# edge_mlp's own term on ScalarE with one row added in PSUM; the attention stages' value sums on TensorE and their keys laid by ScalarE; stage loads in order of need

## The chip, the cores and the metric

One core of a Trainium2 chip runs the whole program in one launch. The metric is the device time of one execution in microseconds (us). The kernel before takes 4426.26 us, the median of three runs (4425.43 to 4427.96).

## What is computed

Four graph layers over 3,125 nodes with 256 features and 53,125 edges, sorted by destination node. `h` is the rectified layer norm of `x`, and each layer adds its result to `x`.

```python
# layer 0: message MLP, node MLP, layer norm
m     = relu(concat([h[src], h[dst], edge_attr]) @ eW1 + eb1) @ eW2 + eb2
agg   = segment_sum(m, dst)
x    += layer_norm(h + relu(concat([h, agg]) @ nW1 + nb1) @ nW2 + nb2)
# layer 1: 4 heads; the key of an edge carries its relation
enh   = h + 0.1 * query_emb
score = sum_d(Q[dst] * (K[src] + 0.2 * rel_w[edge_type])) / 8
w     = softmax over the edges of a destination
x    += layer_norm(segment_sum(w * V[src], dst) @ Wo + bo + h)
# layer 2: 8 heads, a softmax over all edges, key + edge_attr @ We
# layer 3: graph attention with one head, then gates (tanh, sigmoid)
```

## The kernel before

The nodes are ordered and cut into 25 blocks of 128, one node per partition. The edges of a node are taken four at a time: a *step* handles one block with up to four edges ("slots", QE = 4) for each of its 128 nodes. There are 120 steps in each edge stage, 15 turns of a hardware loop with AQ = 8 steps. A step's record (`rec`) holds its block number and the source nodes of its four slots.

The stages run one after the other with a barrier between: lists, tables for layer 0 (`make_tables`), `edge_mlp`, `update_nodes`, `attend` for layer 1, `project_out`, `attend` for layer 2, `share_softmax`, tables for layer 3, `gat_edges`, `gate_nodes`. Five engines run their own written orders, tied only by semaphores; there is no scheduler. `Chain` makes VectorE (DVE) wait for its own last instruction (`step(...)`), or lets it go on and wait later (`put`, `until`). `hold` is a wait and a no-op. In a step GpSimd (POOL) issues indirect DMAs: four gather the source rows of the four slots from a table in HBM (512 values a row) into `ring`, and in `edge_mlp` and layer 2 a fifth gathers edge features. SyncE (SP) loads the records, and waits until a ring slot is free before it does.

`edge_mlp` (lines 1058 to 1171) makes, for each slot, relu(source row + the block's own row + features times `w_edge`) and adds the four into the block's accumulator in `S["big"]`. TensorE (PE) turns the features (L1130, L1131), writes the own row (with bias, 512 wide, in `S["big2"]`) into the slots 0, 1 and 2 of `psX` by a product with the identity (L1135), and adds the feature products (L1142). `psX` has one PSUM bank for each slot. DVE adds the own row of slot 3 (L1161), adds `psX` to the ring two slots at a time (L1163), and rectifies and sums (L1170). ScalarE (ACT) only copies the turned features (L1118).

`attend` (lines 1512 to 1796) keeps a running maximum `m`, sum `l` and weighted values in `S["big"]` for each block. In step k PE makes the edges' keys in `psX[k % 2]` from the turned features (L1688) and adds the gathered keys with the identity (L1693). DVE multiplies them with the queries (L1764), reduces to scores (L1770), masks (L1778), takes the maximum (L1782) and subtracts it (L1786); ACT takes the exponential (L1664). DVE handles the values one step later: the values of step k-1 are weighted by those exponentials (L1708), the old sum is decayed (L1715), and the four weighted rows are added up (L1712, and L1719 twice). ACT also copies turned features (L1638), and in layer 1 builds one-hot relations (L1646, L1649).

`update_nodes` and `project_out` run rounds over 25 blocks; `NextTables` makes the tables of the next layer three rounds behind. Beside that POOL scatters 200 and 115 rows of sorted edge features (L781) and 25 table rows (L1238). SP issues all their loads in one written order.

## Time and profile before

| | |
|---|---|
| median of 3 runs | 4426.26 us |
| the profiled execution, its own time | 4430.56 us |
| its span | 4428.8 us |
| instructions | 52,906 |
| PE, DVE, ACT, POOL busy | 61%, 73%, 16%, 67% |
| mean granted TensorE clock | 0.788 of full speed |

### The profile page before, as it was taken

Reading aid. Unit: us, or ns where it says so; the run is one execution under the profiler, and the core shown is the slowest. Engines: PE = TensorE matmul, PEld = TensorE weight load, DVE = VectorE, ACT = ScalarE, POOL = GpSimd, SP = SyncE. Lnnn points to the kernel's source line nnn. Section 1 sums busy time; section 2 is a strip of 40 time slices with the busy share of each in tenths; the row PEclk is TensorE's granted clock in tenths of the full one; section 3 lists DMA queues with packets and bytes.
Section 4 is the critical chain, followed back from the end, with each engine's and each line's share of the span. In section 5 each row is a group of like instructions: output and inputs, shape, how many; then the busy total and the mean of one; then the engine's idle time right before and its main releaser. Section 6 shows DMA issues by size and latency. Waiting matters only on the chain. (4 is left out here: it accounts for less than half of the span.)

```text
span 4428.8 us, 52906 instructions
## 1 busy us (share of the span) xinstructions
PE 2686.6 (61%) x11454; PEld 1433.4 (32%) x11454; DVE 3253.1 (73%) x7572; ACT 719.6 (16%) x2122; POOL 2983.3 (67%) x2929
## 2 busy tenths in 40 slices
PE   4244578888887799466666656578888853000007
PEld 4144332222222688233233334344444422000004
DVE  7497458888888233489999976499989986666664
ACT  0011100000000233233333322111111102000004
POOL 0577667777765577677777737677777745777772
PEclk8555799999999899777888878787888876555558
DMA  3235346666665333466666733376666643444441
GB/s 159 36 113 156 76 123 179 178 178 171 175 173 147 74 62 61 119 173 172 173 172 175 199 67 69 102 186 185 187 186 186 186 112 78 111 108 108 108 106 40
DMA packets 408930, 594.52 MB, mean 134 GB/s; under 512 B 267146, under 2 KB 273430, under 8 KB 407806
## 3 DMA queue, kind: packets, MB, share of 16 engines
q0 software_dynamic: 185552, 519.27, 42.8%
q1 hardware_dynamic: 223278, 74.01, 7.1%
q8 instruction: 51, 0.84, 0.1%
q14 instruction: 49, 0.40, 0.0%
HBM read 532.97 MB, written 59.26 MB: 134 GB/s over the span
## 5 line engine op out<-in xcount | busy, mean ns | idle before, releaser
L1106 POOL DMA_INDIRECT edge_ring<-tab,edge_rec x480 | 475.8, 991 | 146.2 <-issue 135.2
L1688 PE MATMUL edge_psX<-edge_w_edge,edge_featT 64*128 64x256 f32 x1920 | 440.6, 451 | 196.3 <-DVE edge_prod L1764 193.7
L2028 POOL DMA_INDIRECT state<-tab,edge_rec x480 | 453.8, 945 | 155.7 <-issue 145.9
L1693 PE MATMUL edge_psX<-state,ident 128*128 128x512 f32 x720 | 446.2, 753 | 113.9 <-DMA state<-tab,edge_feat 104.2
L1135 PE MATMUL edge_psX<-state,ident 128*128 x720 | 379.6, 637 | 135.3 <-DVE edge_ring L1163 135.3
L1618 POOL DMA_INDIRECT state<-tab,edge_rec x360 | 351.5, 976 | 159.1 <-issue 102.4
L1688 PEld LDWEIGHTS edge_psX<-edge_w_edge,edge_featT 64*128 64x128 f32 x1920 | 297.7, 216 | 465.5 <-issue 401.3
L1618 POOL DMA_INDIRECT state<-tab,edge_feat x360 | 352.0, 978 | 109.7 <-issue 103.9
L2201 PE MATMUL gate_psA<-ident,gate_w_nat 128*128 128x128 f32 x8 | 2.0, 428 | 632.1 <-DMA gate_w_nat<-in_L_gnn_W_ih 632.1
L1163 DVE TENSOR_TENSOR edge_ring<-edge_psX,edge_ring 128x1024 f32<-128x1024 f32 x240 | 293.8, 1224 | 73.3 <-PE edge_psX L1142 43.4
L781 POOL DMA_INDIRECT sorted_d<-update_row_out,update_row_idx x200 | 237.7, 1189 | 92.3 <-issue 59.4
L1764 DVE TENSOR_TENSOR edge_prod<-edge_psX,state 128x1024 f32<-128x1024 f32 x240 | 293.9, 1225 | 0.0
L1770 DVE TENSOR_REDUCE edge_cat<-edge_prod 128x16 f32<-128x1024 f32 (+1 forms) x240 | 290.7, 1211 | 0.0
L1142 PE MATMUL edge_psX<-edge_w_edge,edge_featT 64*128 64x512 f32 x960 | 273.0, 645 | 0.0
L1693 PEld LDWEIGHTS edge_psX<-state,ident 128*128 128x128 f32 x720 | 153.7, 237 | 254.7 <-DMA state<-tab,edge_feat 123.2
L1664 ACT ACTIVATE edge_psW<-edge_cat 128x20 f32<-128x20 f32 (+1 forms) x240 | 47.6, 198 | 1086.5 <-DVE edge_cat L1786 1086.5
L1675 PE MATMUL edge_psT<-ident,edge_feat 128*64 128x128 f32 (+1 forms) x732 | 149.2, 319 | 120.4 <-ACT edge_feat L1649 97.1
L1135 PEld LDWEIGHTS edge_psX<-state,ident 128*128 128x128 f32 x720 | 118.8, 191 | 319.4 <-DVE edge_ring L1163 166.7
L1708 DVE TENSOR_TENSOR edge_terms<-state,edge_psW 128x1024 f32<-128x1024 f32 x180 | 218.5, 1214 | 0.0
L2201 PEld LDWEIGHTS gate_psA<-ident,gate_w_nat 128*128 128x128 f32 x8 | 1.6, 223 | 632.5 <-DMA gate_w_nat<-in_L_gnn_W_ih 632.5
L532 POOL DMA_INDIRECT state<-in_edge_sr,rank_edge_i x128 | 157.3, 1229 | 49.0 <-issue 43.1
L1103 POOL DMA_INDIRECT edge_feat<-in_edge_attr,edge_rec x120 | 118.7, 989 | 85.4 <-DMA edge_rec<-rec_d 58.9
(439 smaller groups left out, 6362.0 us busy)
## 6 DMA issues: line engine op xcount, KB each, us to landing
sorted_d<-state SPq DMA_DIRECT2D x7, 2380.0 KB
state<-src_rows SPq DMA_DIRECT2D x25, 562.5 KB
state<-low_rows SPq DMA_DIRECT2D x25, 562.5 KB
state<-tab,edge_rec POOLq DMA_INDIRECT x840, 3.0
edge_ring<-tab,edge_rec POOLq DMA_INDIRECT x600, 3.7
update_row_out<-in_edge_attr SPq DMA_DIRECT2D x40, 156.2 KB
edge_rec<-rec_d SPq DMA_DIRECT2D x364, 8.0 KB, 2.8
state<-tab,edge_feat POOLq DMA_INDIRECT x360, 3.7
```

What stands on the lines that cost most here:

```text
L781: pool.indirect_dma_start(out=self.S["sorted_d"][:, :], out_offset=bass.IndirectOffsetOnAxis(ap=self.idx[:, k, j:j + 1], axis=0), in_=self ...
L1106: pool.indirect_dma_start(out=ring[:, k, s, :], out_offset=None, in_=S["tab0"][:, :], in_offset=bass.IndirectOffsetOnAxis(ap=rec[:, k, R_S ...
L1135: pe.matmul(psX[:, 2 * h + i, :], S["ident"][:, :], blk(S["big2"], b), start=True, stop=False)
L1142: last = pe.matmul(psX[:, 2 * h + i, :], featT[lo:lo + ED, k % 2, h, :], w_edge[lo:lo + ED, :], start=(h == 1 and i == 1), stop=True)
L1163: dve.tensor_tensor(both, psX[:, 2 * h:2 * h + 2, :], both, ALU.add).then_inc(s_xr, 1)
L1618: pool.indirect_dma_start(out=ring[k][:, s, :], out_offset=None, in_=S[f"tab{layer}"][:, :], in_offset=node_of(k, s)).then_inc(s_g[k], 16)
L1688: pe.matmul(psX[k % 2][:, s % 2, s // 2, :], featT[lo:lo + ED, k % 4, s // PAIR, :], w_edge[lo:lo + ED, :], start=(s < 2), stop=False, ski ...
L1693: last = pe.matmul(psX[k % 2][:, a, :, :], S["ident"][:, :], ring[k % RING].rearrange("p (c a) f -> p a c f", a=2)[:, a, :, 0:D], start=Fa ...
L1708: return dve.tensor_tensor(terms[:, :, :].rearrange("p s (h d) -> p s h d", h=heads), vals, bc(w[:, 0:QE, :], 3, [P, QE, heads, hd]), ALU. ...
L1764: dve.tensor_tensor(prod[:, :, :].rearrange("p (c a) d -> p a c d", a=2), psX[k % 2][:, :, :, :], blk(S["big"], b)[:, 0:D].unsqueeze(1).un ...
L1770: scored = step.put(dve.tensor_reduce(score[:, 0:QE, :].rearrange("p s h -> p (s h)"), prod[:, :, :].rearrange("p s (h d) -> p (s h) d", d ...
L2028: pool.indirect_dma_start(out=ring[:, k, s, :], out_offset=None, in_=S["tab3"][:, :], in_offset=bass.IndirectOffsetOnAxis(ap=rec[:, k, R_S ...
```

## The change

In `edge_mlp` ACT copies the own row into all four slots of `psX` (SBUF to PSUM, 128x512 each), and waits for DVE's reads of the step before; PE's three identity products with it go. PE now adds slot 0's gathered row with an identity product. DVE adds the other gathered rows into `psX` in place, and rectifies and sums from `psX` straight into the accumulator. PE waits for each slot's own row by itself.

In `attend` ACT copies the gathered keys into `psX[k % 2]` in two halves before PE adds the feature products; the identity products with the keys go. DVE no longer adds up the weighted rows: it writes the weighted values (`terms`) and the decayed sum (`so_far`, in PSUM), PE adds the four rows into `so_far` with identity products, and ACT copies the sum back to `S["big"]`. The weighting of the values of step k-1 now stands ahead of the product of queries and keys of step k. The layer 2 features lie in both halves of the partitions.

`update_nodes` loads by need, with a semaphore for each group; its 25 loads of degrees become one, from a new HBM tensor that `edge_mlp` stores, and DVE's cast of them goes. Eight loads of `rel_w` become two. `project_out` waits for its weights later. The diff, cut to its core:

```diff
@@ edge_mlp, ScalarE
+                act.wait_ge(s_open, 1)
...
+                        for s in range(QE):
+                            if s % 2 == 0:
+                                hold(act, s_xr, t * (2 * AQ) + (2 * q + s // 2 + 1))
+                            act.activation(psX[:, s, :], own, ACT.Copy).then_inc(s_own, 1)
@@ edge_mlp, TensorE
-                            pe.wait_ge(s_xr, t * (2 * AQ) + (2 * q + h + 1))
-                            for i in range(2 - h):
-                                pe.matmul(psX[:, 2 * h + i, :], S["ident"][:, :], blk(S["big2"], b), start=True, stop=False)
...
+                                pe.wait_ge(s_own, t * (QE * AQ) + (QE * q + 2 * h + 1 + i))
+                                last = pe.matmul(psX[:, s, :], featT[lo:lo + ED, k % 2, h, :], w_edge[lo:lo + ED, :],
+                                                 start=False, stop=(s > 0), skip_group_check=True)
                             if h == 0:
+                                pe.wait_ge(s_g[k][0], uses(t, q, RING_0) * 32)
+                                last = pe.matmul(psX[:, 0, :], S["ident"][:, :], ring[:, k, 0, :], start=False, stop=True, skip_group_check=True)
@@ edge_mlp, VectorE
+                        row1 = step.put(dve.tensor_tensor(psX[:, 1, :], psX[:, 1, :], ring[:, k, 1, :], ALU.add))
+                        first = step.put(dve.scalar_tensor_tensor(acc, psX[:, 0, :], 0.0, acc, ALU.max, ALU.add))
...
+                        rows23 = step.put(dve.tensor_tensor(psX[:, 2:4, :], psX[:, 2:4, :], ring[:, k, 2:4, :], ALU.add))
...
+                        second = step.put(dve.scalar_tensor_tensor(acc, psX[:, 1, :], 0.0, acc, ALU.max, ALU.add))
...
+                        step.until(second)
+                        dve.nop().then_inc(s_xr, 1)
+                        step(dve.scalar_tensor_tensor(acc, psX[:, 2, :], 0.0, acc, ALU.max, ALU.add))
+                        step(dve.scalar_tensor_tensor(acc, psX[:, 3, :], 0.0, acc, ALU.max, ALU.add))
+                        dve.nop().then_inc(s_xr, 1)
@@ update_nodes, loads
+                load(eW2[:, :, :], chunks(A[L + "eW2"]), s_w)
+                load(eb2, A[L + "eb2"].rearrange("(a f n) -> a f n", a=1, n=P), s_w)
+                load(deg_row, S["deg_d"].rearrange("(a b n) -> a b n", a=1, n=P), s_w)
...
-                for b in range(NB):
-                    sp.dma_start(deg_row[:, b, :].bitcast(I32), S["lane_d"][b * P:(b + 1) * P, 2].rearrange("(a n) -> a n", a=1),
@@ attend, ScalarE
+                def lay_keys(t, k):
+                    act.wait_ge(s_xr, t * AQ + (k + 1))
+                    act.wait_ge(s_g[k % RING], uses(t, k, RING) * (16 * QE))
+                    for a in range(2):
+                        act.activation(psX[k % 2][:, a, :, :], ring[k % RING].rearrange("p (c a) f -> p a c f", a=2)[:, a, :, 0:D], ACT.Copy).then_inc(s_keys, 1)
+
+                def write_sum(t, k, b):
+                    hold(act, s_sum, t * AQ + (k + 1))
+                    act.activation(blk(S["big"], b)[:, D:D2], so_far, ACT.Copy).then_inc(s_acc, 1)
...
                     for k in range(AQ):
+                        lay_keys(t, k)
                         copy_features(t, k + TURNED)
                         if layer == 1:
                             one_hots(t, k + AHEAD)
+                        write_sum(t, k, b)
+                        if k < AQ - 1:
+                            b = block_of(k, t)
                         act.wait_ge(s_cat, t * AQ + (k + 1))
                         act.activation(w, cat[:, k % 2, :, :], ACT.Exp).then_inc(s_exp, 1)
@@ attend, TensorE
+                        for a in range(2):
+                            pe.wait_ge(s_keys, t * (2 * AQ) + (2 * k + a + 1))
+                            for s in range(a, QE, 2):
...
-                        for a in range(2):
-                            last = pe.matmul(psX[k % 2][:, a, :, :], S["ident"][:, :],
...
+                        add_terms(t, k)
@@ attend, VectorE
+                        hold(dve, s_exp, t * AQ + (k + 1))
+                        weigh(t, k, (k - 1) % RING)
+                        decay(b_prev)
                         dve.wait_ge(s_x, t * AQ + (k + 1))
```

The written order of ACT in one step of `attend` for layer 1. `edge_psW` is the exponentials, `edge_away` and `edge_feat` the one-hots. Before:

```order
L1664 ACTIVATE edge_psW<-edge_cat 128x20
L1637 REGISTER_ALU
L1638 ACTIVATE edge_featT<-edge_psT 128x256
L1646 ACTIVATE edge_away<-iota_c,edge_rec 128x64 x4
L1648 REGISTER_ALU
L1649 ACTIVATE edge_feat<-edge_away,ones 128x256
```

Now, from one exponential to the next:

```order
L1709 ACTIVATE edge_psW<-edge_cat 128x20
L1683 ACTIVATE edge_psX<-state 128x512 x2
L1656 ACTIVATE edge_featT<-edge_psT 128x256
L1668 ACTIVATE edge_away<-iota_c,edge_rec 128x64 x4
L1670 REGISTER_ALU
L1671 ACTIVATE edge_feat<-edge_away,ones 128x256
L1687 ISA
L1687 ACTIVATE state<-edge_psS 128x256
L1677 TENSOR_LOAD edge_rec
L1677 ISA x2
L1709 ACTIVATE edge_psW<-edge_cat 128x20
```

Two copies of keys into `psX` stand right behind the exponential, and the copy of the sum and a register load right ahead of the next.

DVE in the same step, before, from the product of queries and keys (L1764) to the last row of the step (register rows left out are not part of this piece):

```order
L1764 TENSOR_TENSOR edge_prod<-edge_psX,state 128x2x2x256
L1767 ISA
L1767 TENSOR_TENSOR l<-l,edge_psW 128x4
L1708 TENSOR_TENSOR edge_terms<-edge_ring,edge_psW 128x1024
L1769 REGISTER_ALU
L1770 TENSOR_REDUCE edge_cat<-edge_prod 128x16
```

Now, from the weighting of the values on:

```order
L1769 TENSOR_TENSOR edge_terms<-state,edge_psW 128x1024
L1774 ISA
L1774 TENSOR_TENSOR edge_psS<-state,edge_psW 128x256
L1805 ISA
L1805 TENSOR_TENSOR edge_prod<-edge_psX,state 128x2x2x256
L1807 REGISTER_ALU
L1807 TENSOR_TENSOR l<-l,edge_psW 128x4
```

The weighting and the decay moved ahead of the product with the keys.

PE in one step of `edge_mlp`, before (the own row by identity, two slots and one):

```order
L1133 REGISTER_ALU
L1135 ISA
L1135 MATMUL edge_psX<-state,ident 128x512 x2
L1139 REGISTER_ALU
L1142 MATMUL edge_psX<-edge_w_edge,edge_featT 128x512 x2
L1133 REGISTER_ALU
L1135 MATMUL edge_psX<-state,ident 128x512
```

Now, where L1146 is the wait for a slot's own row from ACT and L1150 that for the gathered row:

```order
L1146 ISA
L1147 MATMUL edge_psX<-edge_w_edge,edge_featT 128x512
L1146 REGISTER_ALU
L1147 MATMUL edge_psX<-edge_w_edge,edge_featT 128x512
L1150 REGISTER_ALU
L1151 MATMUL edge_psX<-edge_ring,ident 128x512
L1146 REGISTER_ALU
L1147 MATMUL edge_psX<-edge_w_edge,edge_featT 128x512
```

Each feature product has a wait of its own, and one identity product, of the gathered row, stands where there were three of the own row.

## Rows read from the trace of the kernel before

**Rows 1.** Windows: stretch, busy us (instructions) of PE, PEld, DVE, ACT, POOL, clock.

```profile
590.00:1440.00 850.00, 682.00 (x1930) 217.38 (x1928) 713.07 (x844) 46.08 (x120) 599.20 (x605) 0.98 0.61 169
...
1815.00:2620.00 805.00, 491.96 (x1697) 238.34 (x1698) 701.52 (x1706) 261.72 (x880) 544.21 (x543) 0.80 0.61 166
...
2825.00:3630.00 805.00, 646.92 (x1931) 342.55 (x1931) 703.90 (x1697) 107.71 (x258) 585.72 (x602) 0.82 0.65 178
...
3060.00:3160.00 100.00, 83.34 (x252) 44.45 (x250) 92.85 (x225) 14.20 (x34) 75.97 (x79) 0.85 0.67 188
```

**Rows 2.** One line: ns min/median/max, first and last start; edge_mlp, layers 1 and 2.

```profile
L1163 DVE TENSOR_TENSOR edge_ring<-edge_psX,edge_ring x240: 1223/1224/1226, 615.7 to 1434.4; 128x1024 f32<-128x1024 f32 x120
...
L1764 DVE TENSOR_TENSOR edge_prod<-edge_psX,state x120: 1223/1225/1226, 1831.4 to 2590.7; 128x1024 f32<-128x1024 f32 x120
...
L1764 DVE TENSOR_TENSOR edge_prod<-edge_psX,state x120: 1220/1225/1226, 2853.3 to 3615.6; 128x1024 f32<-128x1024 f32 x120
```

**Rows 3.** Timeline of edge_mlp: start us, us, engine, line, count, idle before.

```profile
1424.00 1.22 DVE L1163 TENSOR_TENSOR edge_ring<-edge_psX,edge_ring 128x1024 f32<-128x1024 f32 x1 [0.22 <-DVE state L1170]
...
1425.37 1.98 PE L1135 MATMUL edge_psX<-state,ident 128*128 x4 [0.44 <-DVE edge_ring L1163]
...
1427.28 1.13 PE L1142 MATMUL edge_psX<-edge_w_edge,edge_featT 64*128 64x512 f32 x4
...
1430.66 1.22 DVE L1163 TENSOR_TENSOR edge_ring<-edge_psX,edge_ring 128x1024 f32<-128x1024 f32 x1 [0.22 <-DVE state L1170]
```

**Rows 4.** Timeline of one step of attend in layer 1.

```profile
2207.66 0.19 ACT L1664 ACTIVATE edge_psW<-edge_cat 128x20 f32<-128x20 f32 x1 [4.00 <-DVE edge_cat L1786]
...
2209.53 1.21 DVE L1708 TENSOR_TENSOR edge_terms<-state,edge_psW 128x1024 f32<-128x1024 f32 x1
...
2209.69 1.14 PE L1688 MATMUL edge_psX<-edge_w_edge,edge_featT 64*128 64x256 f32 x8 [2.67 <-DVE edge_prod L1764]
...
2210.66 1.21 DVE L1770 TENSOR_REDUCE edge_cat<-edge_prod 128x16 f32<-128x1024 f32 x1
...
2211.03 1.88 PE L1693 MATMUL edge_psX<-state,ident 128*128 128x512 f32 x4
```

**Rows 5.** Groups by line: busy us, mean ns of one, idle before.

```profile
L1170 DVE SCALAR_TENSOR_TENSOR edge_psS<-edge_ring,edge_psS 128x512 f32<-128x512 f32 x240 | 166.9, 696 | 8.2
...
L1715 DVE TENSOR_TENSOR edge_psS<-state,edge_psW 128x256 f32<-128x256 f32 x242 | 101.9, 421 | 0.0
...
L1786 DVE TENSOR_TENSOR edge_cat<-edge_cat,m 128x20 f32<-128x20 f32 (+1 forms) x240 | 43.1, 179 | 0.0
...
L1638 ACT ACT_TABLE_LOAD x30 | 38.5, 1283 | 4.8 <-issue 4.8
...
L1404 ACT ACTIVATE update_sumsT<-update_psR 128x512 f32<-128x512 f32 x25 | 14.9, 597 | 44.5 <-DVEq L1254 42.1 <-PE update_psH L1444 1.8
```

**Rows 6.** The same of ScalarE in layer 1's attend.

```profile
L1638 ACT ACTIVATE edge_featT<-edge_psT 128x256 f32<-128x256 f32 x122 | 44.8, 368 | 1.4 <-PE edge_psT L1675 1.3
...
L1664 ACT ACTIVATE edge_psW<-edge_cat 128x20 f32<-128x20 f32 x120 | 22.7, 189 | 420.8 <-DVE edge_cat L1786 420.8
```

**Rows 7.** Two neighbouring stretches of layer 2's attend, columns as in rows 1.

```profile
3222.97:3226.39 3.42, 1.61 (x7) 0.66 (x6) 3.32 (x5) 0.29 (x1) 2.59 (x3) 0.94 0.68 187
3226.39:3229.80 3.41, 3.41 (x7) 1.27 (x6) 2.87 (x12) 0.72 (x2) 2.54 (x3) 0.56 0.69 184
```

**Rows 8.** Timeline, layer 2: four records of identity products at the half clock.

```profile
3611.55 3.67 PE L1693 MATMUL edge_psX<-edge_ring,ident 128*128 128x512 f32 x4 [2.73 <-DMA edge_ring<-tab,edge_feat]
```

**Rows 9.** Timeline: loads of update_nodes and layer 1, POOL behind them.

```profile
1442.68 16.21 SPq L1382 DMA_DIRECT2D state<-lane_d  x25
...
1469.31 1.21 POOL L781 DMA_INDIRECT sorted_d<-update_row_out,update_row_idx  x1 [30.51 <-DMA update_row_idx<-place_i]
...
1799.96 1.07 POOL L1238 DMA_INDIRECT tab<-update_next_row,lane_i  x1 [0.30 <-DVE update_next_row L1289]
...
1806.57 5.73 SPq L1573 DMA_DIRECT2D edge_w_edge<-in_L_gnn_rel_w  x8
```

More of the change, by code:

```diff
@@ L1122, in _ @@
                 pe.wait_ge(s_w, 32)
+                for s in range(QE):
+                    opened = pe.matmul(psX[:, s, :], S["ident"][0:ED, :], w_edge[0:ED, :], start=True, stop=True)
+                opened.then_inc(s_open, 1)
                 n = turns(pe)
                 with nc.Fori(0, n, engines=[pe.engine], hint_back_edge=True) as t:
-                    b = block_of(pe, t, 0)
                     for q in range(AQ):
@@ L1156, in _ @@
                         k, b = q % RING_0, b_next
-                        for h in range(2):
-                            hold(dve, s_g[k][h], uses(t, q, RING_0) * 32)
-                            both = ring[:, k, 2 * h:2 * h + 2, :]
-                            if h == 1:
-                                step(dve.tensor_tensor(ring[:, k, QE - 1, :], ring[:, k, QE - 1, :], blk(S["big2"], b), ALU.add))
-                            dve.wait_ge(s_x, t * (2 * AQ) + (2 * q + h + 1))
-                            dve.tensor_tensor(both, psX[:, 2 * h:2 * h + 2, :], both, ALU.add).then_inc(s_xr, 1)
-                            if h and q < AQ - 1:
-                                b_next = block_of(dve, t, q + 1)
-                            dve.wait_ge(s_xr, t * (2 * AQ) + (2 * q + h + 3))
-                            for s in (2 * h, 2 * h + 1):
-                                to = blk(S["big"], b) if s == QE - 1 else psS[:, :]
-                                so_far = psS[:, :] if s else blk(S["big"], b)
-                                step(dve.scalar_tensor_tensor(to, ring[:, k, s, :], 0.0, so_far, ALU.max, ALU.add))
@@ L1748, in _ @@
                 dve.nop().then_inc(s_xr, 2)
[L1749 to L1750 removed]
+                dve.nop().then_inc(s_terms, 2 * (RING - 1))
+                dve.wait_ge(s_open, 1)
                 n = turns(dve)
@@ L1794, in _ @@
                 step = Chain(dve, s_v, n * CH + PRE)
-                last_values(step, n, 0, RING - 1, block_of(RING - 1))
+                b = block_of(RING - 1)
+                l = blk(S["l"], b)[:, 0:heads]
+                hold(dve, s_exp, n * AQ + 1)
+                weigh(n, 0, RING - 1)
+                decay(b)
+                step(dve.tensor_tensor(l, l, w[:, QE, :], ALU.mult))
+                step(dve.tensor_reduce(tot[:, :], w[:, 0:QE, :].rearrange("p r h -> p h r"), AX.X, ALU.add))
+                step(dve.tensor_tensor(l, l, tot[:, :], ALU.add))
+                dve.nop(nofuse=True)
         ph.close()
```

223 lines of the change are left out of this document (117 added, 106 removed).

## The prediction

> **What bounds the kernel now.** I first cut the span into stages with the windows [rows 1]. Three edge stages hold 2,460 of its 4,429 us, and in each DVE is busy for 84 to 87% of the stretch, PE for 61 to 80%, POOL for 68 to 73%. ACT is nearly idle in them (46, 262 and 108 us). That invites moving work from DVE to ACT and PE. Then I read one line's first and last start for the length of a step [rows 2]. In edge_mlp L1163 runs twice a step, so 239 intervals are 119.5 steps: 818.7/119.5 = 6.85 us. In attend 119 steps take 759.3 and 762.3 us: 6.38 us in layer 1, 6.41 in layer 2.
>
> Two things already stand close behind DVE. One is POOL. In 100 us of layer 2 it issues 79 transfers [rows 1], 1.27 us each. Layer 2 and edge_mlp need five a step, so no step there can be under 6.33 us; layer 1 needs four, and a scatter in five of eight steps of 12 turns, 4.5 on average, or 5.7 us; as a scatter is a longer one (1.21 us, 1.48 from one to the next [rows 9]) I take 5.9. So of DVE's relief at most 0.5 us a step can be kept in edge_mlp and layer 1 and 0.1 in layer 2. The other is PE, whose clock is at 0.98 of full speed in edge_mlp but 0.80 and 0.82 in attend [rows 1]. At present it does not matter much, because the keys of step k are made while DVE works on step k-1: `psX` is double, and in the timeline PE's keys (L1688) start at 2209.69 under DVE's weighting of 2209.53, a step ahead of their reader [rows 4].
>
> **What the change adds to the path.** The order of ACT decides. Each step it now copies keys into `psX` right behind the exponential of the step before, and PE can only add the features after that, and DVE's product (L1764's) only after PE. The exponential in turn needs that product. So ACT, PE and DVE form one ring in attend, with no double buffer in it, although `psX` still has two halves. In edge_mlp it is the same with the own rows: `psX` is single, DVE reads it to the end of a step now (it rectifies from PSUM), and only then may ACT write, PE add and DVE read again.
>
> Price of a copy of 512 columns from SBUF to PSUM: no row shows one. From below it is the 20 columns to PSUM at 0.19 us, and the 256 of L1638 at 0.37 [rows 6]; from the near side L1404, 512 columns from PSUM, 0.60 [rows 5]. By the slope of the two copies from PSUM, (597-368)/256 = 0.89 ns a column, 492 more columns on 0.19 give 0.63. I take 0.63, and 1.2 for two, as neighbours overlap a little; bounds for the pair 0.7 and 1.4. The Trainium skill (ScalarE: Activation LUTs, What ACT_TABLE_LOAD costs) gives 186 ns and 0.833 ns a column, less 93 for a neighbour; by that the pair would take 1.13 and the sum would fall by some 25 us over the three stages.
>
> PE's part, at the full clock: two full products of 512 columns end in 1.98 us and two on half the rows each, which run side by side, in 1.13 [rows 3]. So a stream of 512 columns is 0.85 us and the tail behind the last 0.28; 256 columns are 0.43 (1.14 for two such streams with the tail [rows 4]).
>
> *Attend, one step, from the end of an exponential.* ACT's pair 1.2, hand-over 0.1, PE's last two slots (both on the lower half of the rows, so one after the other) 0.86 + 0.28 = 1.1, hand-over 0.2: DVE's product starts after 2.6. Meanwhile DVE weights the values (1.21) and decays (0.42) [rows 4, 5], done after 1.6, and waits for 1.0. Then the product 1.23, 0.1 (the weighting that covered its latency is gone from there), the reduction 1.21, mask, maximum and subtraction at 0.18 each with a wait apiece 0.75, the exponential with hand-overs 0.24. Sum 6.13. Once a turn ACT also reloads its table (1.28 us [rows 5]), now on the path because the keys stand behind it, and reads the block number: 1.8/8 = 0.22. That makes 6.35, against 6.38 and 6.41. So 1.5 us of adding (L1712, L1719 twice) leaves DVE, and the ring takes it all back: 0 to -7 us a stage. The sums themselves (four streams of 256, as the two of 512 before, 1.9 us [rows 4]) end after some 4.7 us, their copy and the register load after 5.5, which still fits under the 5.9 at which the scores are ready, by 0.4. The skill's same section adds 1.38 us of draining to each load of a table. No row here shows it; if it were paid it would be 1.38/8 x 240 = 41 us on top.
>
> *Edge_mlp, from DVE's second rectification, which frees slots 0 and 1.* Hand-over 0.1, ACT's pair 1.2, 0.1, slot 1's stream 0.85, the identity product 0.85 + 0.28, so the first two slots are ready after 3.4. DVE then adds row 1 and rectifies slot 0 (0.7 each [rows 5], 0.61 when they overlap), adds rows 2 and 3 (1.14 to the next start) and rectifies slot 1 (0.7): 3.06. With 0.1 that is 6.55, and 0.2 for the loop's edge as now (6.66 between the two L1163 [rows 3], 6.85 on average): 6.75, or -12 us.
>
> *Loads.* 25 loads of degrees cost SP 16.2 us ahead of the row loads on which POOL waits [rows 9]; one costs 0.6. POOL then issues 225 transfers from 1469.3 to 1801.0 without a break (1.48 us each), so the stage ends 15.6 us earlier. That the weights are waited for later changes nothing beside it, and in project_out nothing, since POOL's loads keep their place in SP's order. Eight loads of 5.73 us become two before layer 1: -4.3. The store of degrees at the end of edge_mlp stands behind the last record, four steps before the end, so up to 25 us cover it. Together -20.
>
> So at the full clock everything would sum to -12 - 0 - 20, about -32 us.
>
> **The clock.** That is not what I expect to be granted. In attend the clock falls again and again after PE stood: a stretch in which it was busy for 1.61 of 3.42 us is followed by one at the half clock [rows 7], and there four records take 3.67 us where they take 1.88 [rows 4, 8]. In edge_mlp it is 0.98 today with PE busy for 80% [rows 1]. After the change PE's work there is one 512 stream for three, and it stands from the end of slots 2 and 3 until ACT has refilled slots 0 and 1, about 2.5 us of 6.6; that is the gap that attend has now (2.67 before L1688 [rows 4]). So I expect about 0.81 in all three stages, i.e. a share of (1-0.81)/0.5 = 0.38 of the time at half speed. Work done then takes twice as long, so PE loses half of 0.38 of a step of 7 us, 1.3 us a step. How much falls on the path: before, next to none; now the first burst behind each gap is the ring's. In edge_mlp two streams of 0.85 are on it, in attend 0.86 of some 3.5, and the sums as well once they are late by more than 0.4. I take half, 0.67 us; the bounds are none and all. Three stages of 120 steps: 360 x 0.67 = 240 us.
>
> Sum: 4430.6 (the profiled execution) - 32 + 240 = 4639, and as that execution lies 4.3 us over the median, 4635 us.
>
> The Trainium skill (TensorE: Matmul & The Clock Gate, What's actually happening) says that the default is the throttled state and activity releases it. The trace agrees, with 0.50 in the stretch behind a poorly used one [rows 7].
>
> **Rivals.** *The half clock stays off the path.* For it speaks that DVE is busy for 87% of layer 1 at a clock of 0.80 [rows 1], so half-speed work can be covered. Then the sum at the full clock is the result, 4394 us. Against it: the work on DVE that covered it is what the change takes out or puts ahead of the wait.
>
> *POOL becomes the bound.* If a copy takes 0.37 instead of 0.63 (the 256-column row), a ring is 0.5 shorter, 5.9 in attend, and with the clock up POOL decides: edge_mlp 6.33 (-62), layer 1 5.9 (-58), layer 2 6.33 (-10), loads -20: 4276. It decides from a ring under 6.3 us. This is the case on the other side, and all that the move of DVE's work could bring.
>
> *The whole loss is on the path.* 480 instead of 240: 4875. It needs late sums, so ACT's copy of them waits, and the exponential queued behind it waits too, and DVE with it.
>
> *The changes of sign cancel*, a ring at a good clock with a dearer table load: 4426 within its 0.2%.
>
> **How the numbers follow.** My forecast has 0.60, with a range of its own of 4500 to 4790; the clock off the path 0.10, POOL as the bound 0.12, all of the loss 0.12, no change 0.06. A measurement of this kernel can tell about 0.2% (9 us) from no change. Faster 0.22, within 0.2% 0.05, slower 0.73. The range, 4370 to 4820, leaves out most of POOL's case and the far end of the all-loss one.
>
> **What would show it.** The spacing of the product's starts: over 6.9 us in attend, over 7.1 in edge_mlp. DVE's product should be seen waiting for PE, a wait that hardly exists now, and PE's feature products for ACT. The granted clock of edge_mlp should fall from 0.98 to about 0.8, and POOL should wait for records more. POOL's first scatter should come about 15 us earlier after edge_mlp's end. Wrong would be: a clock in edge_mlp over 0.95, a step at 6.4 with POOL busy throughout, or copies of keys under 0.4 us.

## The result, and the profile after

The changed kernel takes 4881.22 us (median of 4 runs, 4878.83 to 4882.97), the kernel before 4427.11 on the same chip (4 runs, 4425.43 to 4430.25). The ratio is 1.1024, with a 95% interval of 1.1005 to 1.1044: slower by 454 us, where 208 were forecast. The profiled execution took 4881.09 us, 4879.3 of it the span. Two executions further down, one of nine of the kernel before (5559.29) and one of eleven of loads_only (4509.62), lie far above their fellows and are in no ratio.

Windows of the three edge stages after the change, columns as in [rows 1] (the last two are the DMA engines' share and GB/s):

```profile
590.00:1710.00 1120.00, 833.48 (x1470) 254.66 (x1468) 542.73 (x726) 314.66 (x601) 573.40 (x607) 0.63 0.47 128
2090.00:2940.00 850.00, 625.68 (x2132) 442.30 (x2130) 574.99 (x1305) 428.04 (x1201) 516.37 (x528) 0.77 0.55 151
3210.00:4060.00 850.00, 623.40 (x2356) 457.28 (x2353) 574.89 (x1297) 298.97 (x719) 554.17 (x586) 0.80 0.59 164
```

DVE was busy for 84 to 87% of each stage before [rows 1]; now it is for 48% of the first and 68% of the others. The work left it, and nothing became faster. PE's clock is the odd column: in attend about as before, in edge_mlp 0.63 where it was 0.98.

One product of each stage, ns of one, first and last start; they answer to [rows 2] ("product" is short for the DVE instruction that first reads what PE made: the adding of a gathered row in edge_mlp, keys times queries in attend):

```profile
L1168 DVE TENSOR_TENSOR edge_psX<-edge_psX,edge_ring x120: 698/700/700, 623.6 to 1701.9; 128x512 f32<-128x512 f32 x120
...
L1805 DVE TENSOR_TENSOR edge_prod<-edge_psX,state x120: 1223/1224/1226, 2089.1 to 2942.9; 128x1024 f32<-128x1024 f32 x120
...
L1805 DVE TENSOR_TENSOR edge_prod<-edge_psX,state x120: 1223/1225/1226, 3204.2 to 4062.6; 128x1024 f32<-128x1024 f32 x120
```

119 intervals each: 9.06, 7.17 and 7.21 us a step, after 6.85, 6.38 and 6.41. From its first product to the first load behind the stage edge_mlp is 262 us longer, the layers 94 and 96. The first product of edge_mlp comes 8 us later, the loads give back 12, and with a small rest that makes the 450 us by which the span grew.

A step of edge_mlp after the change: start us, us, engine, line, count, idle before.

```profile
1303.09 0.70 DVE L1168 TENSOR_TENSOR edge_psX<-edge_psX,edge_ring 128x512 f32<-128x512 f32 x1 [3.95 <-PE edge_psX L1151]
...
1305.00 1.23 DVE L1172 TENSOR_TENSOR edge_psX<-edge_psX,edge_ring 128x1024 f32<-128x1024 f32 x1 [0.62 <-PE edge_psX L1147]
...
1306.14 0.68 DVE L1176 SCALAR_TENSOR_TENSOR state<-edge_psX,state 128x512 f32 x1
...
1307.06 1.12 ACT L1126 ACTIVATE edge_psX<-state 128x512 f32 x2 [1.32 <-DVEq L1180]
...
1307.71 2.59 PE L1147 MATMUL edge_psX<-edge_w_edge,edge_featT 64*128 64x512 f32 x4 [2.39 <-ACT edge_psX L1126]
...
1310.23 2.07 PE L1151 MATMUL edge_psX<-edge_ring,ident 128*128 128x512 f32 x2
...
1312.34 0.70 DVE L1168 TENSOR_TENSOR edge_psX<-edge_psX,edge_ring 128x512 f32<-128x512 f32 x1 [3.95 <-PE edge_psX L1151]
```

Read it as the ring that the prediction described. DVE gives slots 0 and 1 back at 1306.82, and ACT copies its pair from 1307.06 to 1308.18. PE starts at 1307.71, once the first copy is in, goes on when the second is, and the identity product ends at 1312.30. DVE waits 3.95 us for it; before, it stood 0.22 ahead of such a product, and for itself [rows 3]. Two windows of the same step, columns as above:

```profile
1298.90:1303.00 4.10, 4.10 (x8) 1.07 (x7) 0.24 (x1) 1.14 (x3) 0.94 (x1) 0.50 0.48 104
1304.70:1307.70 3.00, 0.62 (x4) 0.20 (x2) 2.51 (x3) 1.03 (x3) 2.39 (x3) 1.00 0.71 183
```

While DVE waits for PE, PE is busy throughout and at the half clock (0.50). While PE has 0.62 us of work in 3.00, it is granted the full clock. The stage's mean of 0.63 hides that: in this step the full clock is given in the pause, where PE has little work. Over the whole stage no record of the identity product was at the full clock: none took under 1061 ns, where edge_busy2 below has 592 (ns min/median/max).

```profile
L1151 PE MATMUL edge_psX<-edge_ring,ident x240: 1061/1140/1222, 621.5 to 1700.8; 128*128 128x512 f32 x120
```

A step of layer 1's attend, which answers to [rows 4]:

```profile
2301.17 1.23 DVE L1805 TENSOR_TENSOR edge_prod<-edge_psX,state 128x1024 f32<-128x1024 f32 x1 [0.57 <-PE edge_psX L1750]
2301.22 3.43 PE L1732 MATMUL edge_psS<-edge_terms,ident 128*128 128x256 f32 x8
...
2304.19 0.18 DVE L1820 TENSOR_TENSOR edge_cat<-edge_cat,m 128x20 f32<-128x20 f32 x1
...
2304.83 0.38 ACT L1687 ACTIVATE state<-edge_psS 128x256 f32 x1 [1.54 <-PE edge_psS L1732]
2305.45 0.19 ACT L1709 ACTIVATE edge_psW<-edge_cat 128x20 f32<-128x20 f32 x1 [0.24 <-issue]
2305.57 1.10 ACT L1683 ACTIVATE edge_psX<-edge_ring 128x512 f32<-128x512 f32 x2
2305.88 1.22 DVE L1769 TENSOR_TENSOR edge_terms<-state,edge_psW 128x1024 f32<-128x1024 f32 x1 [1.40 <-ACT edge_psW L1709]
2306.21 1.65 PE L1750 MATMUL edge_psX<-edge_w_edge,edge_featT 64*128 64x256 f32 x8 [1.56 <-ACT edge_psX L1683]
```

The scores are ready at 2304.37. The exponential starts at 2305.45, since the copy of the sum stands before it on ACT and waits for PE's eight records, 3.43 us at the half clock (1.89 a step earlier, at 2295.42, at the full one). That is the rival's mechanism ("late sums, so ACT's copy of them waits, and the exponential queued behind it"), at work here beside the ring.

### The profile page after: what moved, and what is told of

Same layout as the page of the kernel before. It is cut to its first block and busy times, and to the rows that moved or that the text cites. A ratio compares the mean times of both kernels' runs of the same rounds, so it can differ in the third digit from the quotient of the medians.

```text
span 4879.3 us, 56754 instructions
## 1 busy us (share of the span) xinstructions
PE 3002.5 (62%) x11978; PEld 1822.2 (37%) x11978; DVE 2854.4 (59%) x6725; ACT 1368.8 (28%) x3446; POOL 2927.4 (60%) x2929
## 5 line engine op out<-in xcount | busy, mean ns | idle before, releaser
L1750 PE MATMUL edge_psX<-edge_w_edge,edge_featT 64*128 64x256 f32 x1920 | 445.8, 449 | 466.2 <-ACT edge_psX L1683 466.2
L1732 PE MATMUL edge_psS<-edge_terms,ident 128*128 128x256 f32 x1936 | 714.0, 536 | 5.0 <-DVE edge_psS L1774 5.0
L1147 PE MATMUL edge_psX<-edge_w_edge,edge_featT 64*128 64x512 f32 x960 | 524.1, 1034 | 270.5 <-ACT edge_psX L1126 270.5
L1732 PEld LDWEIGHTS edge_psS<-edge_terms,ident 128*128 128x128 f32 x1936 | 533.5, 289 | 110.9 <-DVE edge_psS L1774 6.3
L1108 POOL DMA_INDIRECT edge_ring<-tab,edge_rec x480 | 454.0, 946 | 146.2 <-issue 145.9
L1750 PEld LDWEIGHTS edge_psX<-edge_w_edge,edge_featT 64*128 64x128 f32 x1920 | 296.7, 204 | 605.5 <-ACT edge_psX L1683 581.7
L1168 DVE TENSOR_TENSOR edge_psX<-edge_psX,edge_ring 128x512 f32<-128x512 f32 x120 | 83.9, 699 | 474.4 <-PE edge_psX L1151 474.4
L1147 PEld LDWEIGHTS edge_psX<-edge_w_edge,edge_featT 64*128 64x128 f32 x960 | 157.7, 280 | 506.7 <-ACT edge_psX L1126 324.4
L1105 POOL DMA_INDIRECT edge_feat<-in_edge_attr,edge_rec x120 | 113.3, 944 | 368.3 <-DMA edge_rec<-rec_d 366.8
L1126 ACT ACTIVATE edge_psX<-state 128x512 f32 x480 | 268.3, 592 | 183.1 <-DVEq L1180 139.6
L1151 PE MATMUL edge_psX<-edge_ring,ident 128*128 128x512 f32 x240 | 248.8, 1141 | 0.0
L1122 ACT ACTIVATE edge_featT<-edge_psT 128x256 f32<-128x256 f32 x120 | 46.1, 384 | 611.5 <-PE edge_psT L1141 583.8
L1612 POOL DMA_INDIRECT edge_feat<-sorted_d,edge_rec x122 | 115.5, 946 | 149.6 <-DMA edge_rec<-rec_d 121.5
```

The lines of the kernel that those rows point to most:

```text
L1108: pool.indirect_dma_start(out=ring[:, k, s, :], out_offset=None, in_=S["tab0"][:, :], in_offset=bass.IndirectOffsetOnAxis(ap=rec[:, k, R_S ...
L1126: act.activation(psX[:, s, :], own, ACT.Copy).then_inc(s_own, 1)
L1147: last = pe.matmul(psX[:, s, :], featT[lo:lo + ED, k % 2, h, :], w_edge[lo:lo + ED, :], start=False, stop=(s > 0), skip_group_check=True)
L1151: last = pe.matmul(psX[:, 0, :], S["ident"][:, :], ring[:, k, 0, :], start=False, stop=True, skip_group_check=True)
L1732: last = pe.matmul(so_far, S["ident"][:, :], terms[:, s, :], start=False, stop=(s == QE - 1), skip_group_check=True)
L1750: last = pe.matmul(psX[k % 2][:, a, s // 2, :], featT[lo:lo + ED, k % 4, s // 2, :], w_edge[lo:lo + ED, :], start=False, stop=True, skip_g ...
```

## Experiments

The kernel before ran beside each group of these runs, at medians of 4427.07 to 4427.82 us, so times are compared across the groups; "less" means under the changed kernel's 4881.22.

**The two parts alone.** edge_only is the kernel before with only the change's edge_mlp, attend_only with only its attend.

```diff
# edge_only, against the kernel before
-def edge_mlp(nc, S, A): ...      # as before
+def edge_mlp(nc, S, A): ...      # as changed, without the store of degrees
# attend_only
-def attend(nc, S, A, layer): ... # as before
+def attend(nc, S, A, layer): ... # as changed
```

> The kernel before with only edge_mlp's part of the change (no store of degrees). If the stage's own ring, at a half clock, makes the loss, its 9.06 us a step stay and the time is 4427 + 262 = about 4690 (4680 to 4700), with the clock of the stage at 0.63. If the stages act on each other (clock, loads), the stage alone would cost clearly less, under 200.

> The kernel before with only attend's part of the change, in both layers. By the sum of the two traces 94 + 96 = 190 us: 4617 (4605 to 4630), with steps of 7.17 and 7.21 us and a clock of 0.77 to 0.80. If a part of that loss came over from edge_mlp, it would be under 150.

Measured: 4696.11 us (ratio 1.0605, 1.0588 to 1.0623), +269, and 4614.17 us (1.0408, 1.0382 to 1.0433), +187. In edge_only the products run from 621.1 to 1700.9, 9.07 us a step at a clock of 0.63; in attend_only a step takes 7.29 and 7.23 (its four runs spread from 4597.24 to 4633.87, and the profiled one is the slowest). Together 456, less what the loads save, where the whole change costs 454: the losses are separate, and by the steps each lies within its own stage.

**PE's gap in edge_mlp filled.**

```diff
+        psI = ph.ps("psI", [P, D2])
...
                         pe.transpose(psT[k % 2][:, P:2 * P], ...).then_inc(s_T, 1)
+                        for i in range(2):        # edge_busy1: range(1)
+                            pe.matmul(psI[:, :], S["ident"][0:ED, :], w_edge[0:ED, :], start=True, stop=True)
                         pe.wait_ge(s_fT, t * AQ + (q + 2))
```

> The changed kernel, with two products of 64 rows and 512 columns more in each step of edge_mlp, into a bank nobody reads, placed where PE stands before ACT's copies. They only add work to PE, 1.7 us a step at the full clock, 3.4 at the half. Theory of the clock: with its gap filled PE is granted the full clock, its streams on the ring take half as long, the step falls from 9.06 to between 6.8 and 7.4, and the time by 200 to 270 us, to 4610 to 4680. Rival, that copies and hand-overs make the ring long and the clock is a bystander: no change to +200 us (4880 to 5080), since the filling at half speed overruns the gap.

Measured: 4610.07 us, a ratio to before of 1.041 (1.0392 to 1.0427), 271 us less than the changed kernel by adding work. The product's starts, and a window of the stage:

```profile
L1171 DVE TENSOR_TENSOR edge_psX<-edge_psX,edge_ring x120: 698/700/700, 620.9 to 1439.2; 128x512 f32<-128x512 f32 x120
...
640.00:1380.00 740.00, 676.60 (x1736) 228.19 (x1738) 477.42 (x651) 285.10 (x544) 514.89 (x545) 0.97 0.62 175
```

6.88 us a step at 0.97, and most steps take 6.64. Its timeline:

```profile
1002.72 1.12 ACT L1127 ACTIVATE edge_psX<-state 128x512 f32 x2 [1.45 <-DVEq L1183]
...
1003.38 1.64 PE L1150 MATMUL edge_psX<-edge_w_edge,edge_featT 64*128 64x512 f32 x4 [0.61 <-ACT edge_psX L1127]
...
1004.95 1.13 PE L1154 MATMUL edge_psX<-edge_ring,ident 128*128 128x512 f32 x2
...
1006.11 0.70 DVE L1171 TENSOR_TENSOR edge_psX<-edge_psX,edge_ring 128x512 f32<-128x512 f32 x1 [2.06 <-PE edge_psX L1154]
```

From ACT's first copy to DVE's product are 3.39 us. Reckoned were 1.2 + 0.1 + 0.85 + 0.85 + 0.28 = 3.28. So the ring's length at the full clock was right, and what the changed kernel pays above it goes with the clock: the edit only adds work to PE.

> As edge_busy2, with one product more a step in edge_mlp instead of two. If the granted clock follows what PE does in its gap, one should give a clock between 0.63 and 0.96 and a step between 9.06 and 6.88: 4650 to 4800. If PE must be without a gap for anything to be gained, the time stays within 30 us of 4881.

Measured: 4799.56 us, but the four runs lie at 4684.48, 4742.42, 4856.69 and 4872.38, so no ratio is given. Two of them lie in the expected 4650 to 4800, and two within 30 us of the changed kernel, as the other theory had it. The profiled one is the fastest, and its steps show how a middle comes about; the steps of the slower ones are not known.

```profile
650.38 0.70 DVE L1171 TENSOR_TENSOR edge_psX<-edge_psX,edge_ring 128x512 f32<-128x512 f32 x1 [2.05 <-PE edge_psX L1154]
657.02 0.70 DVE L1171 TENSOR_TENSOR edge_psX<-edge_psX,edge_ring 128x512 f32<-128x512 f32 x1 [2.05 <-PE edge_psX L1154]
665.56 0.70 DVE L1171 TENSOR_TENSOR edge_psX<-edge_psX,edge_ring 128x512 f32<-128x512 f32 x1 [3.95 <-PE edge_psX L1154]
674.66 0.70 DVE L1171 TENSOR_TENSOR edge_psX<-edge_psX,edge_ring 128x512 f32<-128x512 f32 x1 [3.69 <-PE edge_psX L1154]
681.31 0.70 DVE L1171 TENSOR_TENSOR edge_psX<-edge_psX,edge_ring 128x512 f32<-128x512 f32 x1 [2.06 <-PE edge_psX L1154]
```

A step takes 6.64 us, or 8.5 and then 9.1, three or four short ones to two long ones all through the stage, and none lies between; the changed kernel has none of the short kind (8.5 to 9.4). So the ring has one length at the full clock, 6.64, and one of 8.5 to 9.4 with its burst at the half, by how much of the step's rest is slow too; the changed kernel's mean is 9.06. Why one filling product brings runs as far apart as 188 us is not shown.

**A shorter ring in edge_mlp.**

```diff
                         first = step.put(...)
+                        step.until(first)
+                        step(dve.scalar_tensor_tensor(acc, psX[:, 1, :], 0.0, acc, ALU.max, ALU.add))
+                        dve.nop().then_inc(s_xr, 1)
                         hold(dve, s_g[k][1], uses(t, q, RING_0) * 32)
                         dve.wait_ge(s_x, t * (2 * AQ) + (2 * q + 2))
                         rows23 = step.put(...)
-                        step.until(first)
-                        second = step.put(...)
...
-                        step.until(second)
-                        dve.nop().then_inc(s_xr, 1)
```

> The changed kernel with DVE's order in edge_mlp changed: slot 1 is rectified, and slots 0 and 1 given back, before rows 2 and 3 are added. The ring from giving back to the next product then no longer holds that addition (1.14 to 1.23 us). If only the length of the ring counts, the step falls by 1.1 to 1.9 us (9.06 to 7.2 to 7.9), the time by 130 to 220, to 4660 to 4750. If POOL's transfers or DVE's own work were the limit, nothing would change (4881). The clock, if it is decided by PE's gap, should rise from 0.63 and add to the gain.

Measured: 4563.63 us (1.0303, 1.0285 to 1.032), 318 under the changed kernel, more than expected.

```profile
L1168 DVE TENSOR_TENSOR edge_psX<-edge_psX,edge_ring x120: 699/700/700, 620.8 to 1387.9; 128x512 f32<-128x512 f32 x120
...
640.00:1380.00 740.00, 603.96 (x1380) 202.78 (x1380) 528.53 (x690) 292.09 (x575) 542.46 (x574) 0.86 0.67 183
```

6.45 us a step, 0.4 under the kernel before, at a clock of 0.86. Taken at one clock the addition is worth 1.1 to 1.2 us; 2.6 were gained. The rest I put down to PE's gap, which is shorter too, and the clock that comes back (0.63 to 0.86); no run parts the two. POOL issues 574 transfers in these 740 us, one every 1.29, so its five a step (6.33 by [rows 1]) are next.

**PE's extra row.** In this one the product of the identity that adds row 0 in PSUM (L1151) is undone.

```diff
-                            if h == 0:
-                                pe.wait_ge(s_g[k][0], uses(t, q, RING_0) * 32)
-                                last = pe.matmul(psX[:, 0, :], S["ident"][:, :], ring[:, k, 0, :], ...)
...
-                        row1 = step.put(dve.tensor_tensor(psX[:, 1, :], psX[:, 1, :], ring[:, k, 1, :], ALU.add))
+                        row1 = step.put(dve.tensor_tensor(psX[:, 0:2, :], psX[:, 0:2, :], ring[:, k, 0:2, :], ALU.add))
+                        step.until(row1)
```

> The changed kernel without PE's product of the identity for row 0 in edge_mlp; DVE adds rows 0 and 1 in one instruction (1.22 instead of 0.70 us). DVE gets more work, PE's part of the ring less. Theory of the ring at the half clock: 2.07 us of PE go, 0.5 of DVE and one latency of 0.15 come, the step falls from 9.06 to 7.4 to 8.0 and the time by 130 to 200 us, to 4680 to 4750. If DVE were the limit, as in the kernel before, the time would rise by up to 60 us.

Measured: 4657.69 us (1.0515, 1.0498 to 1.0531), 223.5 under the changed kernel: 7.26 us a step, and the clock still at 0.64. Giving work back to the engine that was to be relieved gains 1.80 us a step. The product on DVE is 0.53 longer (1.233 for 0.700), so 2.3 us went: PE's product at the half clock (2.07) and, for the most part, DVE's wait for slots 2 and 3 (0.62 in the timeline above). The expected gain was somewhat too small.

**Attend: keys ahead, sums behind, a filled gap, keys on PE.** Four edits, each of the changed kernel's attend alone.

```diff
# keys_ahead
-                        lay_keys(t, k)
+                        if k == 0:
+                            lay_keys(t, k)
+                        if k < AQ - 1:
+                            lay_keys(t, k + 1)
# sum_late: the copy of the sum behind the exponential
-                        write_sum(t, k, b)
...
                         act.activation(w, cat[:, k % 2, :, :], ACT.Exp).then_inc(s_exp, 1)
+                        write_sum(t, k, b)
# attend_busy3
-        w = psW[:, 0:ROWS * heads].rearrange(...)
+        w = ph.sb("w_sb", [P, ROWS * heads])[:, :].rearrange(...)
...
                         add_terms(t, k)
+                        for i in range(3):
+                            pe.matmul(psW[:, 0:D], S["ident"][:, :], w_edge[:, :], start=True, stop=True)
# keys_by_pe: lay_keys goes, PE adds the keys behind the features, into the half that DVE has given back
-                        lay_keys(t, k)
...
+                            last = pe.matmul(psX[k % 2][:, a, :, :], S["ident"][:, :],
+                                             ring[k % RING].rearrange("p (c a) f -> p a c f", a=2)[:, a, :, 0:D], ...)
```

> The changed kernel with the keys of step k+1 laid by ACT during step k, before its exponential, into the other half of psX (in seven steps of eight; not over the edge of the loop). Theory, that keys behind the exponential lengthen the ring: DVE's product no longer waits, what is left is weighting and decay 1.6, sums 3.4 at the half clock (1.9 at the full), their copy and the register load 0.8, exponential 0.24, so 5.1 to 6.1 us a step, and POOL is next with 5.9 in layer 1 and 6.33 in layer 2. That takes 200 to 250 us off: 4630 to 4680. Rival, that the ring is held by the sums in front of the exponential alone: the step stays over 6.9 and the gain under 70 us. A third: ACT, which now waits for the rows a step early, holds back its own exponential and the kernel gets slower.

Measured: 4656.81 us (1.0515, 1.0499 to 1.0531), 224 less; 6.27 us a step in both layers.

```profile
2087.00:2832.80 745.80, 496.92 (x2144) 337.38 (x2143) 569.40 (x1310) 423.46 (x1208) 516.69 (x529) 0.86 0.63 172
3093.10:3839.70 746.60, 510.89 (x2384) 360.89 (x2383) 572.48 (x1310) 298.77 (x730) 558.01 (x591) 0.93 0.69 189
```

The windows run from the first to the last product of each layer. Inside a turn the shortest steps take 5.13 and 5.21 us (5.1 was the lower bound expected), most others up to 7.1, and in layer 1 one in most turns up to 8.6. Over the edge of the loop, where the keys still come behind the exponential, a step takes 9.1 to 9.2 for the most part. The mean of layer 2 is POOL's: 591 transfers of 558.01 us, 0.30 apart, fill 735 of the 746.6. That of layer 1 is not: POOL has 529, under 5.7 us a step, and waits for records, and ACT's one-hots stand 53.2 us for records too.

> The changed kernel with ACT's order in attend changed: the exponential first, then the copy of the sum. The last step of the prediction said that sums at the half clock come after the scores and hold the exponential back; in the trace of after the scores are there at 2304.37 and the exponential starts at 2305.45. Without that the exponential comes 0.9 earlier, the copy then stands ahead of the keys (0.4) and of DVE's weighting: a gain of 0.3 to 0.5 us a step, 70 to 120 us, 4760 to 4810. If late sums cost nothing (the keys' path decides anyway) the time is 4880 or up to 90 more.

Measured: 4814.87 us (1.0878, 1.0861 to 1.0895), 66 less: 6.91 and 6.98 us a step. Just under the expected gain, and of its sign; mending the late sums brings about 0.25 us a step of the 0.8. The clock rose with it, from 0.77 and 0.80 to 0.84, and is part of that gain.

> The changed kernel with three products of 256 columns more in each step of attend, behind the sums, where PE stands before the keys, into a bank nobody reads (for which the weights of the exponential lie in SBUF instead of PSUM). 1.3 us more work for PE a step at the full clock. Theory of the clock: the clock rises from 0.77 and 0.80 to over 0.9, the sums take 1.9 instead of 3.4 us, the steps fall to 6.35 to 6.6 as reckoned for the full clock, and the time by 140 to 200 us, to 4680 to 4740. Rival, clock a bystander: 4880 or more.

Measured: 4765.08 us (1.0766, 1.0749 to 1.0782), 116 less, under the expected 140 to 200. Windows from the first product to the last:

```profile
2089.60:2875.90 786.30, 641.81 (x2858) 493.06 (x2858) 577.59 (x1310) 431.55 (x1204) 578.57 (x529) 0.93 0.60 163
3137.90:3949.50 811.60, 661.21 (x3096) 514.02 (x3095) 583.88 (x1310) 309.17 (x728) 625.55 (x591) 0.95 0.63 174
```

The clock came as expected, and inside a turn a step takes 5.80 and 5.89 us, less than the 6.13 reckoned. The mean is 6.61 and 6.82. In layer 2 POOL is why: its 591 transfers took 625.55 us where keys_ahead has 558.01, some of them up to 2.0 us instead of 0.95, and with 0.30 between them they fill 803 of the 811.6 us. What lengthened them isn't settled; the exponentials lay in SBUF here, and that was not tried alone.

> The changed kernel with attend's keys added by PE again, a step ahead as before the change, while the sums stay with PE. It parts the change of attend in two. Theory, that ACT's keys behind the exponential make the ring and PE's sums do not: DVE loses 1.5 us of adding and keeps its keys early, PE works 5.35 us a step and is granted a better clock, the step falls to 5.9 to 6.35 us, the time by 200 to 300 us, to 4580 to 4680. Rival, that the sums are what hurts (late, and in PE's order ahead of the next keys): the step stays over 6.9, 4810 to 4900.

Measured: 4644.73 us (1.0487, 1.0471 to 1.0504), 236.5 less. The sums stayed on PE, so their being there does not hurt by itself; what goes with the keys behind the exponential does. The edit changes the order and the clock at once, and sums at the full clock are not late, so it does not part these two. Steps of 6.16 and 6.25 us, with PE at a clock of 0.95 and 1.00 under its larger load:

```profile
2089.10:2822.30 733.20, 633.67 (x2619) 370.13 (x2618) 572.67 (x1310) 300.50 (x966) 516.24 (x528) 0.95 0.64 175
3083.90:3827.90 744.00, 640.00 (x2858) 387.37 (x2857) 580.58 (x1309) 171.95 (x490) 557.75 (x590) 1.00 0.69 189
```

**The loads alone**: before's edge_mlp and attend in the changed kernel, with the store of degrees and the two loads of `rel_w` kept.

```diff
 # end of edge_mlp's records, on SP, in the kernel before
+                sp.dma_start(S["deg_d"].rearrange("(b p) -> p b", p=P), S["deg_l"][:, :], ...).then_inc(s_degrees, 16)
+                sp.wait_ge(s_degrees, 16)
 # update_nodes
-                for b in range(NB):
-                    sp.dma_start(deg_row[:, b, :].bitcast(I32), S["lane_d"][b * P:(b + 1) * P, 2]...)
+                load(deg_row, S["deg_d"].rearrange("(a b n) -> a b n", a=1, n=P), s_w)
```

> The kernel before with the change's loads alone (one load of degrees instead of 25, two of rel_w instead of eight, weights waited for later). From the two traces: POOL's first scatter of update_nodes comes 12 to 13 us earlier behind the last rectification of edge_mlp, and nothing is gained before layer 1: 4415 (4412 to 4418). As predicted it would be 20 us, 4407.

Measured: 4422.03 us (0.9988, 0.9978 to 0.9997), 5 us less. From the first load of update_nodes to POOL's first scatter it takes 18.7 us here and 18.5 in the changed kernel, against 31.0 before, so 12.4 are saved there. Some 5 us were lost just ahead:

```profile
1413.66 0.39 SPq L1096 DMA_DIRECT2D deg_d<-deg_l  x1
...
1428.77 1.23 DVE L1166 TENSOR_TENSOR edge_ring<-edge_psX,edge_ring 128x1024 f32<-128x1024 f32 x1 [2.48 <-DMA edge_ring<-tab,edge_rec]
...
1433.22 0.69 DVE L1164 TENSOR_TENSOR edge_ring<-edge_ring,state 128x512 f32<-128x512 f32 x1 [1.65 <-DMA edge_ring<-tab,edge_rec]
...
1464.80 1.21 POOL L781 DMA_INDIRECT sorted_d<-update_row_out,update_row_idx  x1 [18.21 <-DMA update_row_idx<-place_i]
```

Behind the store DVE waits for gathered rows (of the stage's DMA waits of L1166, 2.5 us in all, this is the one), and the last two steps take 8.9 and 9.7 us instead of 6.7: 5.2 us. The store was not taken out by itself, but edge_busy1, edge_busy2, edge_early and both_rings, which store too, also have a step of 9.9 to 10.5 us among their last two in edge_mlp, and edge_only, which does not store, has none; nor have rows_by_dve and the changed kernel, which store and take 7.3 and 9.06 us a step.

**Both mends together**: edge_early and keys_ahead in one kernel, both edits as above.

> The changed kernel with both mends: edge_mlp's slots 0 and 1 given back early, and attend's keys laid a step ahead. If the two losses are separate, as the two parts of the change were, the gains add: 4881 - 318 - 224 = 4339 (4325 to 4355), 2% under the kernel before, with steps of 6.45, 6.27 and 6.27 us. POOL is then what is left (five transfers of 1.25 in 6.33). If a gain in one stage is paid in another (clock, transfers), 4400 or more.

Measured: 4335.35 us (5 runs, 4333.8 to 4340.38), a ratio of 0.9792 (0.9778 to 0.9806) to the kernel before, 92 us under it.

```profile
L1168 DVE TENSOR_TENSOR edge_psX<-edge_psX,edge_ring x120: 699/700/700, 621.7 to 1386.3; 128x512 f32<-128x512 f32 x120
...
L1807 DVE TENSOR_TENSOR edge_prod<-edge_psX,state x120: 1216/1218/1225, 1771.6 to 2511.5; 128x1024 f32<-128x1024 f32 x120
...
L1807 DVE TENSOR_TENSOR edge_prod<-edge_psX,state x120: 1216/1218/1226, 2770.5 to 3517.1; 128x1024 f32<-128x1024 f32 x120
```

6.43, 6.22 and 6.27 us a step: the gains add to within 4 us. This is the change's own division of work; only two places of the code stand elsewhere.

## Where the prediction was right and where it failed

**The ring in edge_mlp at the full clock**: forecast 6.75 us, measured 6.88 on average with the gap filled and 6.64 for most steps. Right; the 0.2 for the loop's edge isn't there (6.65 at that place), and the clock's remaining dips make up the mean.

**The clock in edge_mlp**: this is the step that failed. "So I expect about 0.81 in all three stages", and of PE's loss "I take half, 0.67 us; the bounds are none and all". The trace has 0.63, and the runs show that 2.42 us a step came onto the path, more than the bound "all" (1.3) allowed: the ring goes from 6.64 to 9.06 us. PE's written part (0.85 + 0.85 + 0.28 = 1.98) doubles, and DVE waits 0.62 for slots 2 and 3, 2.6 together where the whole burst is slow. Two faults went in. The gap was forecast well (about 2.5 us; PE stands 2.39), but attend's clock was taken over with it; why such a gap leaves attend at about 0.80 and edge_mlp at 0.63 no run shows. (The forecast also read 0.50 for the stretch behind a poorly used one; [rows 7] has 0.56.) And the loss was worked out as a share of time, as if the half clock fell anywhere. It falls on PE's burst and the full clock on its pause. By the forecast's own working 0.63 is a share of 0.74 of 9.06 us at the half clock, so PE lost 3.35 us a step where 1.3 was said, and 0.72 of that lay on the path where half was taken. With 2.2 us a step instead of 0.57 net, edge_mlp cost 262 where the forecast has (7.42 - 6.85) x 120 = 68. That is 194 of the 246 us missed; attend cost 190 where the sum has 160, the loads gave 12 at the scatters for 20, and the first product came 8 later. Working the written ring out a second time with PE's part doubled would have given 6.75 + 1.98 = 8.7 us a step, most of the 9.06.

**The ring in attend**: forecast 6.35 + 0.67 = 7.02, measured 7.17 and 7.21: near, but in part by luck, as errors cancel. Inside a turn the ring at the full clock is 5.80 to 5.89, not 6.13. At the turn's edge the step takes 9.5 and 9.4 us in the two layers, 2.6 above the others; 1.8 a turn was reckoned. Before, the edge cost 2.0 (7.9 against 5.9) with the table load off the path. ACT's table loads in layer 1, a group by line (busy us, mean ns, idle before):

```profile
L1683 ACT ACT_TABLE_LOAD x15 | 19.2, 1283 | 9.5 <-issue 9.5
```

Each is 1.28 long with 0.63 idle ahead of it (4.8 us over 30 before, 0.16 each [rows 5]). The sums, which were to fit by 0.4, are late at the half clock, as said for that case.

**ACT's copies**: 1.10 to 1.12 for the pair, 1.2 taken. A single one takes 0.58 to 0.60, where 0.63 was reckoned. The Trainium skill's figures (ScalarE: Activation LUTs, What ACT_TABLE_LOAD costs) gave 1.13 for the pair; the trace agrees with 1.12. The 1.38 us of draining that the same section adds is not there: at most the 0.63 us idle ahead of the 1.28.

**Loads**: forecast -20, measured -5 by themselves. The scatters start 12.4 earlier, not 15.6, since SP takes longer over what is left: 9.6 us from its first load for the next tables to the rows' indices, 7.2 before. "Up to 25 us cover" the store was wrong: on SP it is hidden, but the gathers beside it land late, and two steps pay 5.2. Before layer 1 nothing is gained in the changed kernel (362.1 us from first scatter to first product, as before).

**The rivals.** POOL as the bound needed cheaper copies, by the forecast. Its pace was reached without them, from the order alone: layer 2 of keys_ahead and both_rings is held by POOL at 6.27 us a step, and edge_mlp (6.43) and layer 1 (6.22) are near it in both_rings. The whole loss on the path (4875, 0.12) is within 6 us of the time, but with another split: 1.3 us a step in each stage was said, and it was 2.2, 0.8 and 0.8. Its point of decision, late sums, holds in attend (sum_late) and has no part in edge_mlp. What would show the mechanism was seen, but for the clock (0.63 where about 0.8 was named): DVE's product waits for PE (474.4 us in edge_mlp, where L1163 had 43.4 before, the first line below), PE's feature products for ACT (270.5 and 466.2), POOL for its records (366.8 before L1105 alone):

```profile
L1163 DVE TENSOR_TENSOR edge_ring<-edge_psX,edge_ring 128x1024 f32<-128x1024 f32 x240 | 293.8, 1224 | 73.3 <-PE edge_psX L1142 43.4 <-DVE state L1170 24.6
...
L1750 PE MATMUL edge_psX<-edge_w_edge,edge_featT 64*128 64x256 f32 x1920 | 445.8, 449 | 466.2 <-ACT edge_psX L1683 466.2
...
L1147 PE MATMUL edge_psX<-edge_w_edge,edge_featT 64*128 64x512 f32 x960 | 524.1, 1034 | 270.5 <-ACT edge_psX L1126 270.5
...
L1168 DVE TENSOR_TENSOR edge_psX<-edge_psX,edge_ring 128x512 f32<-128x512 f32 x120 | 83.9, 699 | 474.4 <-PE edge_psX L1151 474.4
L1105 POOL DMA_INDIRECT edge_feat<-in_edge_attr,edge_rec x120 | 113.3, 944 | 368.3 <-DMA edge_rec<-rec_d 366.8
```

## What to carry to other kernels

Moving work off the busiest engine cost 10% here, and paid 2% once the engines that took it no longer had to wait for the one that they serve. Before counting what an engine sheds, follow its buffer around: who frees it, who fills it, who reads it. When TensorE is on such a ring and pauses in it, work the ring out twice, with its burst at each level of the clock; the mean granted clock of the stage did not say what the burst got. A first remedy is to free the buffer one instruction earlier or fill the other half a step ahead, not to move the work back.

## What the runs showed of the hardware that was not expected

- Products that nobody reads made the kernel 271 us faster: two a step took edge_mlp from 9.06 to 6.88 us, its clock from 0.63 to 0.97.
- With one such product the same kernel on the same chip took 4684 to 4872 us in four executions; in the fastest its steps are either 6.64 or 8.5 to 9.1 us long.
- More work in the same time gave the better clock also where the work was real: keys_by_pe has PE busy for 86% of both layers' stretches at 0.95 and 1.00, the changed kernel for 74 and 73% at 0.77 and 0.80. But PE's busy share does not order the clocks: keys_ahead has 67 and 68% at 0.86 and 0.93, with the changed kernel's work in less time, and a half clock makes busy time longer.
- Where edge_mlp ended with a store of 12.5 KB in four-byte elements, the last two steps of loads_only took 5.2 us more, two of its instructions waiting for gathered rows.
